# Attention's tiles in another order: scores and values in threes instead of twos

## The reference

```python
q, k, v = ...                       # 2 batches, 2048 positions, 16 query heads, 8 key heads, width 64
log_G = cumsum(log_sigmoid(6.906768 + gate))          # a decay per key head
s = einsum('bthd,bshd->bhts', q, k) * d ** -0.5
logits = 2 * log(abs(s) + 1e-30) + log_G[:, :, :, None] - log_G[:, :, None, :]
a = exp(logits - rowmax(logits)), causal              # so: squared scores times a decay
y = einsum('bhts,bshd->bthd', a, v) / (sum(a) + 1e-6)
y = (y - mean) / sqrt(var + 1e-9) * ln_w, then @ w_proj
```

## Time and profile before

| | |
|---|---|
| median of 3 runs | 2249.56 us |
| profiled execution, its own time | 2256.52 us |
| its span (first to last instruction) | 2254.8 us |
| attention, first score matmul to last maximum transposes | about 335.6 to 1414 us |
| PE, DVE, ACT busy over the whole span | 89%, 80%, 57% |
| one pair in the middle of the attention | 65.90 us |

### The profile page before, as it was taken

The page is one execution under the profiler, slowest core; times in us unless marked ns, Lnnn a source line. Parts: engine busy times, 40 slices in busy tenths (PEclk is TensorE's granted clock), DMA queues, the critical chain, the costliest instruction groups (busy, mean ns, idle before and its releaser), DMA issues. The chain is left out here.

```text
span 2254.8 us, 37911 instructions
## 1 busy us (share of the span) xinstructions
PE 2013.7 (89%) x13199; PEld 1376.1 (61%) x13199; DVE 1792.6 (80%) x2636; ACT 1296.5 (57%) x2168; POOL 797.6 (35%) x745
## 2 busy tenths in 40 slices
PE   7787847999999999999999999699924999999994
PEld 5565633444444444444444444499823999999994
DVE  5666656999999999999999999677768777777773
ACT  4333326777777777777777776244410666656562
POOL 3666640111111111101111111166616566666663
PEclk9989878999999999999999999699955999999997
DMA  5666559333444433344443330344441344434444
GB/s 186 230 209 207 195 197 221 78 87 90 122 117 117 120 76 86 95 122 117 117 115 78 88 96 19 102 130 129 121 140 35 76 85 88 85 85 88 81 85 107
DMA packets 156104, 260.57 MB, mean 116 GB/s; under 512 B 44568, under 2 KB 120160, under 8 KB 149472
## 3 DMA queue, kind: packets, MB, share of 16 engines
q1 hardware_dynamic: 127792, 214.07, 34.0%
q0 software_dynamic: 15840, 22.29, 6.2%
q10 hardware_dynamic: 12304, 22.02, 3.0%
HBM read 162.40 MB, written 100.14 MB: 116 GB/s over the span
## 5 line engine op out<-in xcount | busy, mean ns | idle before, releaser
L984 ACT ACTIVATE att_sb_a<-att_ps_s,att_sb_fg,att_sb_f 128x1024 f32<-128x1024 f32 x384 | 459.2, 1204 | 283.3 <-PE att_ps_s L1121 267.4
L1022 DVE TENSOR_TENSOR keep_sb_store<-keep_sb_store,att_sb_a 128x1024 f32<-128x1024 f32 (+1 forms) x528 | 533.7, 1038 | 35.1 <-ACT att_sb_a L984 33.0
L940 POOL TENSOR_SCALAR_AFFINE_SELECT att_sb_dec<-att_sb_dec 128x128 f32<-128x128 f32 x256 | 131.5, 514 | 937.9 <-ACT att_sb_dec L974 937.9
L1140 PE MATMUL att_ps_off<-att_sb_a,att_sb_v 128*64 128x512 f32 x1520 | 389.0, 601 | 0.3 <-DVE att_sb_part L1049 0.3
L1121 PEld LDWEIGHTS att_ps_s<-keep_sb_late,att_sb_k 64*128 64x128 f32 x1920 | 158.7, 185 | 159.1 <-issue 86.8
L1121 PEld LDWEIGHTS att_ps_s<-att_sb_q,att_sb_k 64*128 64x128 f32 x1896 | 156.3, 185 | 156.3 <-issue 86.4
L1773 ACT ACTIVATE ffn_sb_h<-ffn_ps_p,ffn_sb_b_cols 128x256 f32<-128x256 f32 x320 | 152.0, 477 | 173.2 <-PE ffn_ps_p L1964 131.9
L1121 PE MATMUL att_ps_s<-keep_sb_late,att_sb_k 64*128 64x512 f32 (+3 forms) x1920 | 247.2, 381 | 0.0
L1121 PE MATMUL att_ps_s<-att_sb_q,att_sb_k 64*128 64x512 f32 (+2 forms) x1896 | 242.6, 380 | 0.0
L1038 DVE SCALAR_TENSOR_TENSOR att_sb_a<-att_ps_s,att_sb_dec 128x1024 f32<-128x1024 f32 (+3 forms) x256 | 210.1, 821 | 40.2 <-PE att_ps_s L1121 35.2
L1878 DVE TENSOR_TENSOR ffn_sb_h_lo<-ffn_sb_h,ffn_sb_h_hi 128x256 fp32r<-128x256 f32 x320 | 213.1, 709 | 33.4 <-ACT ffn_sb_h_hi L1766 22.6
(11 more groups left out here) (257 smaller groups left out, 3670.7 us busy)
## 6 DMA issues: line engine op xcount, KB each, us to landing
q_rows<-early_sb_halves SPq DMA_DIRECT2D x32, 1024.0 KB, 4.1
att_sb_k<-k_rows SPq DMA_DIRECT2D x60, 512.0 KB, 16.0
ffn_sb_raw<-L_ffn_W ACTq DMA_DIRECT2D x36, 512.0 KB
close_sb_nT<-num_rows SPq DMA_DIRECT2D x34, 512.0 KB, 4.0
k_rows<-early_sb_halves SPq DMA_DIRECT2D x16, 1024.0 KB, 4.8
keep_sb_late<-q_rows SPq DMA_DIRECT2D x32, 512.0 KB, 14.0
num_rows<-att_sb_num SPq DMA_DIRECT2D x64, 256.0 KB, 2.4
att_sb_hb<-half_log SPq DMA_DIRECT2D x15, 1024.0 KB, 22.9
```

The lines of the kernel that those rows point to most:

```text
L940: nc.gpsimd.affine_select(out=tile, in_=tile, compare_op=ALU.is_ge, fill=0.0, base=0, pattern=[[1, P]], channel_multiplier=-1).then_inc(de ...
L984: nc.scalar.activation(x, s_ps[slot(op)][:, :, :], ACT.Square, scale=f[:, p, i - 1, s:s + 1], bias=fg[:, p, i - 1, s:s + 1]).then_inc(sq_d ...
L1022: nc.vector.tensor_tensor(x[:, :, c:TB], x[:, :, c:TB], y[:, :, c:TB], ALU.max).then_inc(max_done, 1)
L1140: last = nc.tensor.matmul(ps[h * HD:(h + 1) * HD, c:TB], v_tile, a[:, a_slot(op), h, c:TB], start=(s == 0), stop=(s == (ST * i if kind == ...
```

## The change

`PATTERN` is another list of the same 44 places (of each word as many as before), and values are placed by a new function. They fall behind every third place, so that PE does the scores of three places and then the values due. The least distance is 2 places for off and 5 for diag tiles. Where a block's first values would stand in the same group as the last values of the block that held the bank before, they and what follows go one group later. All other offsets are new too. At the start of the first pair the waits for the loads are put at the first tile that needs each of them.

```diff
-PATTERN = ("o1 d3 o1 d3 x0 o1 d3 o1 d3 "
...
+PATTERN = ("d3 o1 o1 d3 o1 d3 d3 o1 o2 o2 o2 d1 o2 x0 x3 "
...
+GROUP, OFF_LAG, DIAG_LAG = 3, 2, 5
...
+def values_places(place):
+
+
+    at = {}
+    for kind, lag in (("off", OFF_LAG), ("diag", DIAG_LAG)):
+        block, last = None, 0
+        for op in sorted((op for op in place if op[1] == kind), key=place.get):
+            d = place[op] + lag
+            d += (GROUP - 1 - d) % GROUP + 0.5
+            if block not in (None, (op[0], op[2])) and d <= last:
+                d = last + GROUP
+            block, last = (op[0], op[2]), max(d, last)
+            at[op] = last
+    return at
...
     def values_at(op):
-        d = place[op] + (2.5 if op[1] == "off" else 5.5)
-        return d if int(d) % 2 else d + 1
+        return at_values[op]
 
     def max_at(op):
         if op[1] == "off":
-            return place[op] + 1.8 if op[3] else place[op[:3] + (1,)] + 1.79
-        return place[op] + 4.8
+            return place[op] + 2.25 if op[3] else place[op[:3] + (1,)] + 2.24
+        return place[op] + 4.81
...
-    sq_order = Order({op: place[op] + (0 if op[1] == "off" else 2.2) for op in offs + diags})
-    dec_order = Order({op: place[op] - 5 for op in diags})
-    et_order = Order({(q, i): place[q, "off", i, 0] + 0.5 for q, i in blocks})
+    sq_order = Order({op: place[op] + (0 if op[1] == "off" else 2.96) for op in offs + diags})
+    dec_order = Order({op: place[op] - 5.95 for op in diags})
+    et_order = Order({(q, i): place[q, "off", i, 0] - 1.18 for q, i in blocks})
...
-    own_order = Order({op: place[op] + 0.3 for op in diags})
-    row_order = Order({op: place[op] + 0.6 for op in maxes})
+    own_order = Order({op: place[op] + 0.34 for op in diags})
+    row_order = Order({op: place[op] - 0.11 for op in maxes})
...
-    part_order = Order({(q, i): values_at(last_off(q, i)) + 1.2 for q, i in blocks})
-    total_order = Order({(q, i): values_at(last_own(q, i)) + 1.2 for q, i in owns})
+    part_order = Order({(q, i): values_at(last_off(q, i)) + 0.55 for q, i in blocks})
+    total_order = Order({(q, i): values_at(last_own(q, i)) + 0.29 for q, i in owns})
...
-                if kind == "off" and s == 0:
-                    if q == 0 and i == 1:
-                        pe.wait_ge(first.part_in, FIRST_PART)
-                    elif q == 0 and i == 2:
-                        pe.wait_ge(first.some_in, FIRST_SOME)
-                    elif i == (1 if q else 3):
-                        arrived(pe, q)
+                if q and kind == "off" and i == 1 and s == 0:
+                    arrived(pe, q)
+                if op == first_use[0]:
+                    pe.wait_ge(first.part_in, FIRST_PART)
+                if op == first_use[1]:
+                    pe.wait_ge(first.some_in, FIRST_SOME)
+                if op == first_use[2]:
+                    arrived(pe, 0)
```

More of the change, by code:

```diff
@@ L746 @@
 GUARD = 1e-15
-PATTERN = ("o1 d3 o1 d3 x0 o1 d3 o1 d3 "
-           "o2 o2 d1 o2 d1 o2 x3 o2 d1 o2 d1 o2 o2 "
-           "o3 d2 o3 d2 o3 x1 o3 d2 o3 d2 o3 o3 d0 o3 d0 x2 o3 o3 d0 o3 d0 o3")
+PATTERN = ("d3 o1 o1 d3 o1 d3 d3 o1 o2 o2 o2 d1 o2 x0 x3 "
+           "o2 d1 o2 o2 d1 o2 d1 o3 d2 o3 o3 d2 d2 o3 o3 "
+           "d2 d0 o3 x1 o3 o3 o3 o3 d0 d0 x2 d0 o3 o3")
 CARRIED = ("d3", "x3", "x0")
+GROUP, OFF_LAG, DIAG_LAG = 3, 2, 5
 def attention_places():
@@ L800, in last_own @@
         return (q, "diag", i, ST - 1)
+    at_values = values_places(place)
     def values_at(op):
-        d = place[op] + (2.5 if op[1] == "off" else 5.5)
-        return d if int(d) % 2 else d + 1
+        return at_values[op]
     def max_at(op):
         if op[1] == "off":
-            return place[op] + 1.8 if op[3] else place[op[:3] + (1,)] + 1.79
-        return place[op] + 4.8
+            return place[op] + 2.25 if op[3] else place[op[:3] + (1,)] + 2.24
+        return place[op] + 4.81
     blocks = [(q, i) for q in range(PAIRS) for i in OFFS]
@@ L824, in attend @@
+    total_order = Order({(q, i): values_at(last_own(q, i)) + 0.29 for q, i in owns})
     slots = Order({op: place[op] for op in offs + diags})
     pe_todo = [(place[op], "s", op) for op in place] + [(values_at(op), "av", op) for op in offs + diags]
[L827 to L830, removed]
+    act_todo = [(place[op] + (0 if op[1] == "off" else 2.96), "sq", op) for op in offs + diags]
@@ L831, in attend @@
+    act_todo += [(place[op] - 5.95, "dec", op) for op in diags]
+    act_todo += [(place[q, "off", i, 0] - 1.18, "et", (q, i)) for q, i in blocks]
+    act_todo += [(q * N + N * 0.88, "factors", (q + 1,)) for q in range(PAIRS - 1)]
     dve_todo = [(max_at(op), "max", op) for op in offs + diags]
-    dve_todo += [(place[op] + 0.3, "own", op) for op in diags]
-    dve_todo += [(place[op] + 0.6, "row", op) for op in maxes]
+    dve_todo += [(place[op] + 0.34, "own", op) for op in diags]
+    dve_todo += [(place[op] - 0.11, "row", op) for op in maxes]
@@ L834, in attend @@
     dve_todo += [(max_at(last_off(q, i)) + 0.01, "scale", (q, i)) for q, i in blocks]
-    dve_todo += [(values_at(last_off(q, i)) + 1.2, "part", (q, i)) for q, i in blocks]
-    dve_todo += [(values_at(last_own(q, i)) + 1.2, "total", (q, i)) for q, i in owns]
+    dve_todo += [(values_at(last_off(q, i)) + 0.55, "part", (q, i)) for q, i in blocks]
+    dve_todo += [(values_at(last_own(q, i)) + 0.29, "total", (q, i)) for q, i in owns]
     pe_todo.sort(), act_todo.sort(), dve_todo.sort()
@@ L1082, in _ @@
         def _(pe):
+            in_part = {(0, "off", 1, s) for s in range(ST)}
+            in_some = {(0, "off", 2, s) for s in range(2 * ST)} | {(0, "diag", 1, s) for s in range(ST)}
+            scored = [op for op in s_order if op[0] == 0 and op[1] != "max"]
+            first_use = [next(op for op in scored if op in in_part), next(op for op in scored if op in in_some),
+                         next(op for op in scored if op not in in_part | in_some)]
+            first_full = next(op for op in av_order if op[0] == 0 and op not in in_part)
             def wait_slot(user):
@@ L1135, in values @@
                     v_tile = first.v_part[:, s, :]
-                elif q == 0 and s == 0 and kind == "off" and i == 2:
+                elif op == first_full:
                     pe.wait_ge(first.v_in, 16)
```

## The result

The changed kernel takes 2199.56 us (median of 4 runs, 2198.79 to 2199.75) against 2249.41 us for the kernel before (4 runs). The ratio is 0.978, 95% interval 0.9763 to 0.9797: faster by 50 us. I had forecast 2213 and a range from 2200 to 2234; the time lies 0.4 us under it. The direction held, the size was more than a quarter too small: 36 us forecast, 50 measured.

The account below looks back on a forecast made before the run. PE was taken to bound the attention, with DVE close behind. Fewer turns -42.3, more waits +5, the end +1 gave -36 us: from a median of 2249.6 to 2213 us, range 2200 to 2234.

Parts of the forecast that it names:

- a turn costs 0.36 us: Each PE switch between scores and values in the attention loses 0.36 us; fewer turns save 42.3 us together.
- The distance between a score tile and the next user of its PSUM tile gets longer: On PE, the shortest such distance grows from 2.4 to 2.8 us to mostly 3.7 us.
- The end, +1: In the last pair, the reductions of blocks 0 and 3 close the stage one behind the other: 1 us more.
- I add 0.9 us per pair to PE's sum for the places where one waits for the other: Waits between PE and DVE were to grow from 0.6 to 0.9 us per pair, giving 63.6 us a pair.
- The two engines are level: In the attention DVE needs 62.5 to 63.5 us per pair, against PE's new sum of 62.7 us.
- The split reduction, 2.2 us in every third pair: Where PE splits the reductions of blocks 0 and 3, DVE stands still 2.2 us, 0.75 us per pair on average.
- The banks, "it goes; nothing else is late there": PE's 0.2 us wait per pair for DVE to empty a values bank disappears, worth 3 us at most.
- "No gain": Rival: the third tile pays as if it had its own turn, or DVE's waits all stay; 2245 to 2254, chance 0.07.
- "Slower": Rival: groups of three fill all three PSUM tiles, DVE frees them late, later scores start late; 2278 us, chance 0.09.
- DVE did not take over: Rival that DVE takes over: 3.6 to 4.7 us of its waits per pair stay; about 2232 us, chance 0.18.
- the 11 doubled max places: Transposes of two maxima in succession on PE: up to 0.15 us each saved or lost, 1.7 us; counted as 0.

Follow-up runs that it names:

- e2: The changed kernel's list and offsets, but groups of two instead of three: ratio 0.9972 to the kernel before.
- e16: Kernel before plus one unused 1.1 us DVE reduction per pair, ahead of block 0's 384 wide diag tile, where DVE waited for scores: ratio 1.0003.
- e17: Kernel before plus the same unused 1.1 us DVE reduction per pair, behind the scaling of block 2, ahead of the instruction emptying the bank: ratio 1.0078.
- e3: Changed kernel with a block's first values right behind the last ones of the block that held the bank, not one group later: ratio 1.0008 to the kernel before.
- e15: Changed kernel with only the ends of blocks late again in DVE's order (offsets 1.2 and 1.2): ratio 0.9988 to the kernel before.
- e9: Changed kernel with groups of four instead of three: ratio 1.0035 to the kernel before.
- e12: As e1, but with the ends of blocks earlier in DVE's order (0.55 and 0.29 instead of 1.2): ratio 0.9838 to the kernel before.
- e14: Kernel before, groups of two, with only the ends of blocks earlier in DVE's order (0.55 and 0.29 instead of 1.2): ratio 0.9995.
- e1: Changed kernel with the list and all offsets of the kernel before, values still in groups of three: ratio 1.0011 to the kernel before.

## Why the prediction was wrong

Its steps, one by one:

- *PE is the bound, and a turn costs 0.36 us*: right. The sum fell by 42.8 us, the third tile cost 0.69, the prices held to 0.02 us per group. e2 repeats it at a small size (5.7 by the sum, 6.3 measured, within 3).
- *The distance between a score tile and the next user of its PSUM tile gets longer*: right. No matmul waits in the three pairs shown, and DVE's waits for scores fell from 2.1 to 0.3 us per pair.
- *The end, +1*: about right. Per pair the rest above the sum fell from 0.6 to 0.15 us, 7 to 8 us over 16 pairs, and in all it fell by 6.9, so the two ends together cost at most 1. It was not measured by itself.
- *"I add 0.9 us per pair to PE's sum for the places where one waits for the other"*: wrong, and it is nearly the whole miss. Measured are 0.15 us: the waits went from 0.6 to 0.15 us per pair where I let them grow to 0.9. 16 x 0.75 = 12 us, of the 13 by which the forecast was too high.
- *"The two engines are level"*: this is the reason behind it, and it does not hold. Both engines' sums being near does not make them wait. The idle time of DVE, as a sum, was neither a reserve nor a debt: e16 and e17 differ by 17 us with the same work, and in the three pairs shown the changed kernel runs without a wait of PE at 2.6 us of idle DVE time per pair. What counts is what stands ahead of the instructions that PE waits for.
- *The split reduction, 2.2 us in every third pair*: the place was right, the size not. It is 0.49 us in the trace (682.13 above), because DVE comes late to the first reduction (679.83, while the transposes started at 677.03) and has the end of the block in between. The 2.2 us were computed as if DVE were on time for the first reduction.
- *The banks, "it goes; nothing else is late there"*: it went, but I put its worth at 3 us and saw it as a small extra. e3 and e15 show that without the rule, or without the early ends, 47 to 51 us return. Of the new offsets I named only those of ACT, and did not weigh the two that decide. That the wait went was right for a reason that does not suffice, the group of scores in between, which e15 has too; here the forecast was lucky.
- *The rivals*: none came about. "No gain" did not, since the third tile cost 0.69. "Slower" named the three PSUM tiles as what would bite; that happens in fours (e9), not in threes. DVE did not take over: three pairs took 188.26 us with DVE at 180.6, and PE's sum gave the time. The Trainium skill (TensorEngine Tiling (Array Packing), PSUM Bottleneck), which I had set against the full gain, says that after a fourfold speedup of PE the reading of PSUM may become the bound; here, where the two heads of a score tile share the rows, DVE comes near and does not.

What stays open: how the 13 us between e12 and the changed kernel split between the list and the other offsets. And that the early ends are worth nothing in twos and 39 to 47 us in threes because the bank is needed again sooner is read from the orders and from the places of the waits (e14, e1); no run changed that distance by itself.

## What to carry to other kernels

Where matmuls of different shapes alternate, price a turn from two groups of the timeline that differ by one tile, and count turns in the order: that sum was right to 2 us in 43. Then look, for each bank that is used again, at what stands ahead of the instruction that empties it on its own engine. Two sort keys there were worth as much as all the turns, and the idle time of that engine, summed, did not tell it. An edit of such keys is a test only where it moves an end whose bank is needed soon: compare the orders first.

## What the runs showed of the hardware

A turn between matmuls with 64 contraction rows and those with 64 output columns costs 0.36 us in pairs, also in groups of three, with PE at its full granted clock: 0.21 us belong to a group of scores and 0.15 to a group of values. Which part of the turn costs this time was not tried. Transposes behind transposes cost 0.88 us for the second eight (1.90 us for sixteen) against 1.02 for eight alone, so they too lose about 0.15 us per group. I had counted nothing for it; over the 11 doubled max places it is 1.5 us, of which the 42.8 above has 0.5.

The timeline of PE in the changed kernel where two max places follow each other:

```profile
805.56 1.97 PE L1126 MATMUL att_ps_s<-keep_sb_ident,keep_sb_store 128*128 128x128 f32 x16
807.46 0.73 PE L1147 MATMUL att_ps_s<-keep_sb_late,att_sb_k 64*128 64x512 f32 x4
```

From 805.56 to 807.46 are the 1.90 us of two turned maxima.
